# Output stage of full attention: gate folded into the output weights, normalising on ScalarE, loops written out

## The chip, the cores and the metric

The kernel runs on one core of a Trainium2 chip. The metric is the device time of one execution in microseconds, as the median of several runs. The engines are named as in the profile: PE is TensorE (PEld its weight loads), DVE is VectorE, ACT is ScalarE, POOL is GpSimd, and SP is SyncE, which here issues every DMA. PE's clock has two levels, 1.2 and 2.4 GHz; the profile gives the granted share.

## The reference

All is float32. B = 8 batches of N = 1024 tokens with D = 256 channels. The reference is a block with adaptive layer norm: full attention, then two layers of windowed attention with feed-forward. The change lies in the line that ends the full attention and in the norm behind it:

```python
mod = (_silu(c) @ wmod).reshape(8, 6, 1, -1)
sa, ca, ga, sb, cb, gb = (mod[:, i] for i in range(6))
ga = (2 * (ga >= 0) - 1) * jnp.maximum(jnp.abs(ga), 0.25)
h = _layernorm(x) * (1 + ca) + sa
x = x + ga * (softmax(q @ k.T / 4) @ v @ wo.T)   # attention(h), 16 heads of 16
h = _layernorm(x) * (1 + cb) + sb
```

Each batch b has one gate row ga[b] of 256 numbers, one scale row and one shift row, which are the rows 2, 4 and 3 of mod_d[b].

## The kernel before

The program is a chain of stages, each a block of its own with a barrier at its end: setup, projections, full_attention, attention_out, and then twice window_attention and feed_forward. The change lies in attention_out alone. It takes the attention's result att_d and the input x from memory, and writes x1 (the sum above) and the normalised, modulated h, in two halves lo and hi.

The tokens go through in NC = 16 chunks of 512 (CT = 4 tiles of 128 tokens, each 128 partitions by 256 channels); two chunks make a batch. For a chunk n:

- SP loads at (attention), xt (input) and mrow (three rows of mod_d, copied to all 128 partitions) into one of R = 4 buffers. After the first four chunks a load waits for POOL's last operation of chunk n - 4. SP then stores x1 when it is summed, and lo and hi when POOL is done.
- PE turns the attention (L1053, transposes, at to pT), ACT copies it out of PSUM (L1073, pT to aT), and PE multiplies by the output weights w["wo"] (L1061, to pY). pT, aT and pY have one buffer each: the product of chunk n waits until DVE has read pY of chunk n - 1, and the copy of chunk n until the product of chunk n - 1 is done.
- DVE multiplies pY by the gate row (L1085, gate) and adds the input (L1089, add). Both are placed inside the layer norm of the chunk before. That norm has steps chained by a semaphore: statistics (L364), aggregation (L369), variance plus epsilon (L371), then a reciprocal root by ten small steps on 128x4 values (L82, and three rounds of L84, L86, L87). After it come four normalising operations (L1101), one for each tile.
- POOL multiplies by the scale row and adds the shift row (L1136, twice 128x1024), from xn to hm.

The order on each engine is written by hand in body(n, r). On DVE that is: norm of chunk n up to the sixth step, gate of n + 1, two steps, add of n + 1, the last steps, normalize of n. The engines run four chunks written out, then an engine loop (Fori) of four chunks for each turn; DVE and SP also write out the last four.

Of the kernel before, what the change touches and what calls it, by code (L numbers as in the profile page):

```python
# [30 lines left out]
CT = 4  # L31
# [937 lines left out]
def attention_out(nc, x, ident, w, mod_d, att_d, x1_d, lo_dst, hi_dst):  # L969


    with ExitStack() as ctx:
# [15 lines left out]
        stats, mv = sb("ao_stats", [P, CT, 6]), sb("ao_mv", [P, CT, 2])  # L988
        ve, rstd, tmp = sb("ao_ve", [P, CT]), sb("ao_rstd", [P, CT]), sb("ao_tmp", [P, CT])
# [7 lines left out]
        gated = sig("gated", 2)  # L997
        chain = sig("chain", LN_INCS)
        normed = sig("normed")
# [9 lines left out]
        def drive(eng, body):  # L1009
            for n in range(R):  # L1010
                body(n, n)
            with eng.Fori(1, NC // R) as i:
                for r in range(R):
                    body(i * R + r, r)

        with nc.Block() as block:
            @block.sync
            def _(sp):
                def load(n, p):
                    if not isinstance(n, int):  # L1020
# [12 lines left out]

                for n in range(R):
                    load(n, n)
                with sp.Fori(0, NC // R - 1) as i:
                    for r in range(R):
                        store(i * R + r, r)
                        load(i * R + R + r, r)
                for n in range(NC - R, NC):  # L1040
                    store(n, n % R)
                for n in range(NC - R, NC):
                    sp.wait_ge(stored.sems[n % R], stored.upto(n))

            @block.tensor
            def _(pe):
                def body(n, r):
                    pe.wait_ge(loaded.sems[r], loaded.upto(n))
                    if again(n):
                        pe.wait_ge(aT_ready.sem, aT_ready.upto(n - 1))  # L1050
                    for t in range(CT):
                        for k in range(KT):
                            last = nc.tensor.transpose(pT[:, k, t * P:(t + 1) * P],  # L1053
                                                       at[:, r, t, k * P:(k + 1) * P], ident[:])
# [10 lines left out]
                drive(pe, body)  # L1065

            @block.scalar
            def _(act):
                def body(n, r):
                    act.wait_ge(turned.sem, turned.upto(n))  # L1070
                    if again(n):
                        act.wait_ge(projected.sem, projected.upto(n - 1))
                    nc.scalar.copy(aT[:], pT[:]).then_inc(aT_ready.sem, 1)  # L1073

                drive(act, body)

            @block.vector
            def _(dve):
                def gate(n, r):
                    dve.wait_ge(loaded.sems[r], loaded.upto(n))  # L1080
                    dve.wait_ge(projected.sem, projected.upto(n))
                    if not (isinstance(n, int) and n < R):
# [4 lines left out]
                def add(n, r):  # L1087
                    dve.wait_ge(gated.sem, gated.upto(n, 1))
                    nc.vector.tensor_tensor(x1[:, r], x1[:, r], xt[:, r], ALU.add).then_inc(gated.sem, 1)  # L1089

                def stats_of(n, r, steps):
                    if steps[0] == 0:
                        dve.wait_ge(gated.sem, gated.upto(n))
                    layer_norm_steps(nc, dve, chain, n, steps, x1[:, r], stats, mv, ve[:], rstd[:], tmp[:])

                def normalize(n, r):
                    dve.wait_ge(chain.sem, chain.upto(n))
                    if later(n):
                        dve.wait_ge(modded.sem, modded.upto(n - 2))
# [3 lines left out]
                    last.then_inc(normed.sem, 1)  # L1103

                def body(n, r, following=True):
# [10 lines left out]
                gate(0, 0)  # L1116
                add(0, 0)
                for n in range(R):
                    body(n, n)
                with dve.Fori(1, NC // R - 1) as i:  # L1120
                    for r in range(R):
                        body(i * R + r, r)
                for n in range(NC - R, NC):
                    body(n, n % R, following=n + 1 < NC)

            @block.gpsimd
            def _(pool):
                def body(n, r):
                    p = r % 2
                    pool.wait_ge(normed.sem, normed.upto(n))  # L1130
                    for t_in, t_out, row, op in ((xn, xn, 2, ALU.mult), (xn, hm, 1, ALU.add)):
                        if row == 1:
                            pool.wait_ge(modded.sem, modded.upto(n, 1))
                            if later(n):
# [3 lines left out]
                                                op).then_inc(modded.sem, 1)  # L1138

                drive(pool, body)  # L1140
# [939 lines left out]
```

## Time and profile before

| | us |
|---|---|
| median of 3 runs | 4590.83 |
| lowest and highest | 4581.98, 4592.19 |
| profiled execution, its own time | 4591.15 |
| its span in the trace | 4589.3 |
| attention_out in it, from the last DMA of the stage ahead to the first of the next | 1711.6 to 1901.7 |

The profiled execution's own time is 1.85 us more than its span and 0.3 us above the median. Over the whole program PE is busy for 91% of the span, DVE 79%, ACT 61% and POOL 35%; but these shares are means over stages of very different kinds, and attention_out is 4% of the span. So the stage has to be read by itself: the views of the trace are cut to its stretch, and times are counted from the span's start.

### The profile page before, as it was taken

The page shows a single profiled execution, that of the slowest core. Times are in us where ns is not written, and L with a number is a line of the kernel's source. Part 1 is how long each engine was busy: PE and PEld are TensorE (multiplying, and loading weights), DVE is VectorE, ACT ScalarE, POOL GpSimd, SP SyncE. Part 2 cuts the span into 40 slices and gives each one's busy share as a digit, 9 for nine tenths or more (in the row PEclk, how much of TensorE's full clock was granted, in tenths as well). Part 3 has the DMA queues.
Part 4 walks back from the last instruction along what each step waited for, and adds up shares of the span by engine and source line. Part 5 has one row for each costly group of instructions (what it writes and reads, how often), then busy time and mean ns, then how long its engine had stood idle before and what let it go on. Part 6 is the DMA issues. An engine that isn't in the chain of part 4 may idle for free. (4 is left out here: it accounts for less than half of the span.)

```text
span 4589.3 us, 81912 instructions
## 1 busy us (share of the span) xinstructions
PE 4160.5 (91%) x27034; PEld 2652.0 (58%) x27034; DVE 3603.7 (79%) x7996; ACT 2779.6 (61%) x6209; POOL 1597.4 (35%) x2408
## 2 busy tenths in 40 slices
PE   5959999999999976499999996999799999987998
PEld 2423333333333325377777775888577777766887
DVE  5679999999999938688888885565588888875665
ACT  1428888888888861166767664444467666653343
POOL 2400000000000003356555553444455555644555
PEclk8969999999999977799999998999899999998999
DMA  5943343343342307400000001111100000002221
GB/s 194 371 94 55 51 63 54 53 62 52 56 62 49 58 22 230 147 25 27 27 25 27 24 20 57 51 52 44 57 27 26 26 27 24 27 13 87 86 69 54
DMA packets 368553, 295.62 MB, mean 64 GB/s; under 512 B 66364, under 2 KB 325432, under 8 KB 368192
## 3 DMA queue, kind: packets, MB, share of 16 engines
q1 hardware_dynamic: 368192, 291.11, 25.8%
q8 instruction: 190, 3.11, 0.3%
q14 instruction: 171, 1.40, 0.1%
HBM read 178.74 MB, written 111.21 MB: 63 GB/s over the span
## 5 line engine op out<-in xcount | busy, mean ns | idle before, releaser
L885 ACT ACTIVATE fa_P<-fa_pS 128x512 f32<-128x512 f32 x2048 | 1111.8, 595 | 327.7 <-PE fa_pS L811 279.0
L912 DVE TENSOR_REDUCE fa_mx<-fa_pR 128x2 f32<-128x1024 f32 x1024 | 1205.6, 1221 | 92.4 <-PE fa_pR L792 78.0
L1519 POOL TENSOR_TENSOR wa_pn<-wa_pr,wa_ri 128x512 f32<-128x512 f32 (+1 forms) x512 | 673.4, 1315 | 506.9 <-DVE wa_ri L1576 506.3
L1452 ACT ACTIVATE wa_pr<-wa_sm,wa_mn 128x256 f32<-128x256 f32 (+1 forms) x1024 | 496.9, 488 | 172.1 <-DVE wa_mn L1567 149.5
L1136 POOL TENSOR_TENSOR ao_xn<-ao_xn,ao_mod 128x1024 f32<-128x1024 f32 x16 | 37.5, 2347 | 1598.7 <-DVE ao_xn L1101 1598.7
L826 PE MATMUL fa_pO<-fa_P,fa_V 128*32 128x512 f32 x4096 | 554.6, 614 | 0.0
L811 PE MATMUL fa_pS<-fa_Q,fa_K 50*128 50x512 f32 x2048 | 512.1, 497 | 41.5 <-ACT fa_P L885 11.2
L811 PEld LDWEIGHTS fa_pS<-fa_Q,fa_K 50*128 50x128 f32 x2048 | 192.8, 185 | 525.4 <-ACT fa_P L885 438.4
L792 PE MATMUL fa_pR<-fa_K,fa_Q 48*128 48x512 f32 x2048 | 430.1, 463 | 57.3 <-DMA fa_K<-parts_d 38.4
L1302 PE MATMUL wa_pQK<-wa_wqkv,wa_xT 128*128 128x512 f32 x1536 | 420.8, 410 | 6.3 <-DVE wa_qa L1613 6.3
L1567 DVE CUSTOM_DVE_ANT_0 wa_sm<-wa_pS,wa_mask 128x256 f32<-128x256 f32 (+1 forms) x1024 | 357.1, 403 | 21.3 <-issue 16.0
L1462 ACT COPY wa_pT<-wa_pP 128x512 f32<-128x512 f32 (+1 forms) x512 | 285.5, 558 | 127.3 <-PE wa_pP L1349 127.2
L1925 POOL TENSOR_TENSOR ff_u<-ff_uF,ff_u 128x512 fp32r<-128x512 f32 x192 | 246.7, 1289 | 307.3 <-ACT ff_u L2038 306.3
L2030 ACT ACTIVATE ff_gl<-ff_pG,ff_b 128x512 f32<-128x512 f32 x192 | 131.8, 687 | 355.9 <-PE ff_pG L1970 355.6
L792 PEld LDWEIGHTS fa_pR<-fa_K,fa_Q 48*128 48x128 f32 x2048 | 195.8, 188 | 247.1 <-DVE fa_mx L912 152.2
L1349 PE MATMUL wa_pP<-ident,wa_pn 128*128 128x128 f32 x1920 | 310.2, 282 | 15.1 <-ACT wa_pT L1462 10.9
L1970 PE MATMUL ff_pG<-ff_hT,ff_w 128*128 128x512 f32 x1152 | 302.6, 398 | 23.0 <-DVE ff_w L1899 23.0
L1302 PEld LDWEIGHTS wa_pQK<-wa_wqkv,wa_xT 128*128 128x128 f32 x1536 | 272.7, 191 | 54.0 <-DVE wa_qa L1613 7.7
L1336 PE MATMUL wa_pS<-wa_kT,wa_qT 64*128 64x256 f32 (+1 forms) x2048 | 277.0, 387 | 7.5 <-DVE wa_mn L1567 2.2
L1984 PE MATMUL ff_pY<-ff_w,ff_u 128*128 128x256 f32 x2304 | 279.7, 281 | 0.0
L1984 PEld LDWEIGHTS ff_pY<-ff_w,ff_u 128*128 128x128 f32 x2304 | 274.3, 188 | 0.2
L1361 PE MATMUL wa_pO<-wa_pT,wa_V 128*64 128x128 f32 x3840 | 268.4, 281 | 4.3 <-ACT wa_pT L1462 4.3
(186 smaller groups left out, 7058.7 us busy)
## 6 DMA issues: line engine op xcount, KB each, us to landing
parts_d<-pj_parts SPq DMA_DIRECT2D x64, 512.0 KB, 5.3
fa_Q<-parts_d SPq DMA_DIRECT2D x192, 128.0 KB, 4.5
fa_K<-parts_d SPq DMA_DIRECT2D x192, 128.0 KB, 7.4
v_d<-pj_v SPq DMA_DIRECT2D x16, 1024.0 KB, 8.4
fa_V<-v_d SPq DMA_DIRECT2D x32, 512.0 KB, 9.8
pj_x<-in_L_attn_x SPq DMA_DIRECT2D x16, 512.0 KB, 7.6
fa_Q<-fa_nrow SPq DMA_DIRECT2D x512, 2.0 KB
att_d<-fa_att SPq DMA_DIRECT2D x64, 128.0 KB, 2.3
```

The lines of the kernel that those rows point to most:

```text
L792: last = nc.tensor.matmul(slot[:, e, :], Qs[at:at + SROWS, s, a, q * P:(q + 1) * P], Ks[at:at + SROWS, s, a, kh * HALF:(kh + 1) * HALF], s ...
L811: nc.tensor.matmul(pS[:, (s * exped.per + u + e) % T, :], Ks[at:at + SROWS + 2, s, a, kb * P:(kb + 1) * P], Qs[at:at + SROWS + 2, s, a, ha ...
L826: last = nc.tensor.matmul(pO[h * 32:(h + 1) * 32, :], V[:, s, kb, h, :], Pr[:, k % 2, h, :], start=(kb == 0), stop=(kb == KB - 1))
L885: nc.scalar.activation(Pr[:, k % 2, h, :], pS[:, (s * exped.per + u) % T, :], ACT.Exp).then_inc(exped.sem, 1)
L912: nc.vector.tensor_reduce(mx[:, q // QB, :, a, q % QB, kh], row_slot(), AX.X, ALU.max).then_inc(row_free, 1)
L1302: last = nc.tensor.matmul(out, xT[:, x, k, :], wqkv[:, y, k, j * INNER:(j + 1) * INNER], start=(i == 0), stop=(i == len(products) - 1))
L1349: last = nc.tensor.transpose(pP[:, at:at + P], pn[:, hp % 2, hh, side * WIN:(side + 1) * WIN], ident[:])
L1452: last = nc.scalar.activation(pr[:, hp % 2, hh, lo:], sm[:, hp % 2, hh, lo:], ACT.Exp, bias=mn[:, p, h:h + 1], scale=-1.0, accum_out=rs[:, ...
L1519: nc.gpsimd.tensor_tensor(pn[:, hp % 2, :, lo:], pr[:, hp % 2, :, lo:], inv, ALU.mult).then_inc(s["weighted"].sem, 1)
L1567: last = nc.vector.tensor_tensor_reduce(out=sm[:, hp % 2, hh, lo:], in0=pS[:, hh, (hp % 2) * 2 * WIN + lo:(hp % 2 + 1) * 2 * WIN], in1=mas ...
L1970: last = nc.tensor.matmul(ps[:, j % 2, :], w1[:, x, k, part, j * P:(j + 1) * P], hT[:, p, y, k, :], start=(i == 0), stop=(i == len(product ...
L1984: last = nc.tensor.matmul(pY[:, t, :], u[:, x, j, t * P:(t + 1) * P], w2[:, y, j, :], start=(j == 0 and i == 0 and t % 2 == 0), stop=(j == ...
```

## The change

The gate row is multiplied into the output weights. One DMA at the start of the stage brings all eight gate rows to every partition (grow, 128 x 2048 numbers, 1 MB), and POOL makes wg, the weights of a batch times its gate row (weigh, 128x512), for two batches ahead of the chunks and then for one batch after each second chunk. PE's product reads wg in place of w["wo"] and also waits for it. DVE's gate is gone, and its add reads pY and xt. The load of mrow takes two rows in place of three.

The four normalising operations are gone from DVE. In their place one small operation (offset) makes shift = -mean * rstd, and ACT computes xn = rstd * x1 + shift in four activations of 128x256. On ACT they stand behind the copy of the next chunk: copy of n, then normalize of n - 1. mv, rstd and shift have two buffers.

All the engine loops of the stage are written out.

```diff
-        mrow = sb("ao_mod", [P, R, 3, D])
+        mrow = sb("ao_mod", [P, R, 2, D])
+        grow = sb("ao_gate", [P, B, D])
+        wg = sb("ao_wg", [P, 2, KT, D])
...
-        def drive(eng, body):
-            for n in range(R):
-                body(n, n)
-            with eng.Fori(1, NC // R) as i:
-                for r in range(R):
-                    body(i * R + r, r)
+        def drive(body):
+            for n in range(NC):
+                body(n, n % R)
...
-                    src = mod_d[bass.ds(n // 2, 1), 2:5, :].to_broadcast([P, 3, D])
+                    src = mod_d[bass.ds(n // 2, 1), 3:5, :].to_broadcast([P, 2, D])
...
+                sp.dma_start(grow[:], mod_d[:, 2, :].rearrange("(o b) c -> o b c", o=1).to_broadcast([P, B, D])
+                             ).then_inc(gates, 16)
...
+                    pe.wait_ge(weighed.sem, weighed.upto(n // 2))
                     if again(n):
-                        pe.wait_ge(gated.sem, gated.upto(n - 1, 1))
+                        pe.wait_ge(gated.sem, gated.upto(n - 1))
                     for t in range(CT):
                         for k in range(KT):
-                            last = nc.tensor.matmul(pY[:, t, :], aT[:, k, t * P:(t + 1) * P], w["wo"][:, k, :],
+                            last = nc.tensor.matmul(pY[:, t, :], aT[:, k, t * P:(t + 1) * P], wg[:, n // 2 % 2, k, :],
...
                     nc.scalar.copy(aT[:], pT[:]).then_inc(aT_ready.sem, 1)
+                    if n > 0:
+                        normalize(n - 1, (n - 1) % R)
+
+                def normalize(n, r):
+                    act.wait_ge(shifted_by.sem, shifted_by.upto(n))
+                    if n >= 2:
+                        act.wait_ge(modded.sem, modded.upto(n - 2))
+                    for t in range(CT):
+                        last = nc.scalar.activation(xn[:, r % 2, t, :], x1[:, r, t, :], ACT.Identity,
+                                                    bias=shift[:, r % 2, t:t + 1], scale=rstd[:, r % 2, t:t + 1])
+                    last.then_inc(normed.sem, 1)
...
-                    row = mrow[:, r, 0, :].unsqueeze(1).to_broadcast([P, CT, D])
-                    nc.vector.tensor_tensor(x1[:, r], pY[:], row, ALU.mult).then_inc(gated.sem, 1)
+                    nc.vector.tensor_tensor(x1[:, r], pY[:], xt[:, r], ALU.add).then_inc(gated.sem, 1)
...
-                    for t in range(CT):
-                        last = nc.vector.tensor_scalar(xn[:, r % 2, t, :], x1[:, r, t, :], mv[:, t, 0:1],
-                                                       rstd[:, t:t + 1], ALU.subtract, ALU.mult)
+                    nc.vector.scalar_tensor_tensor(out=shift[:, r % 2], in0=mv[:, r % 2, :, 0], scalar=-1.0,
+                                                   in1=rstd[:, r % 2], op0=ALU.mult,
+                                                   op1=ALU.mult).then_inc(shifted_by.sem, 1)
...
                     stats_of(n, r, range(0, 6))
-                    if following:
-                        gate(n + 1, (r + 1) % R)
-                    stats_of(n, r, range(6, 8))
-                    if following:
+                    if n + 1 < NC:
                         add(n + 1, (r + 1) % R)
-                    stats_of(n, r, range(8, LN_INCS))
-                    normalize(n, r)
+                    stats_of(n, r, range(6, LN_INCS))
+                    offset(n, r)
...
+                def weigh(b):
+
+                    if b >= 2:
+                        pool.wait_ge(projected.sem, projected.upto(2 * b - 3))
+                    nc.gpsimd.tensor_tensor(wg[:, b % 2], w["wo"][:], grow[:, b].unsqueeze(1).to_broadcast([P, KT, D]),
+                                            ALU.mult).then_inc(weighed.sem, 1)
```

How this moves instructions is seen best on two engines. On ACT, at the start of the stage, there stood copies alone before:

```order
L1073 COPY ao_aT<-ao_pT 128x1024 [waits ao_turned]
L1073 COPY ao_aT<-ao_pT 128x1024 [waits ao_projected,ao_turned] x3
```

Now it reads:

```order
L1077 COPY ao_aT<-ao_pT 128x1024 [waits ao_turned]
L1077 COPY ao_aT<-ao_pT 128x1024 [waits ao_projected,ao_turned]
L1086 ACTIVATE ao_xn<-ao_x,ao_shift,ao_rstd 128x256 [waits ao_shifted_by]
L1086 ACTIVATE ao_xn<-ao_x,ao_shift,ao_rstd 128x256 x3
L1077 COPY ao_aT<-ao_pT 128x1024 [waits ao_projected,ao_turned]
L1086 ACTIVATE ao_xn<-ao_x,ao_shift,ao_rstd 128x256 [waits ao_shifted_by]
```

The third copy (chunk 2) now stands behind the four activations of chunk 0, and these wait for DVE's offset of chunk 0 (the semaphore ao_shifted_by).

On DVE, the piece of the difference for one chunk (here chunk 1) from its first statistics on:

```order
 L364 BN_STATS ao_stats<-ao_x 128x6 x4
 L367 MEMSET ao_tmp 128x4
...
 L84 SCALAR_TENSOR_TENSOR ao_tmp<-ao_rstd 128x4
 L86 TENSOR_TENSOR ao_tmp<-ao_tmp,ao_ve 128x4
-L1085 TENSOR_TENSOR ao_x<-ao_pY,ao_mod 128x1024
+L1100 TENSOR_TENSOR ao_x<-ao_pY,ao_x 128x1024
 L87 SCALAR_TENSOR_TENSOR ao_rstd<-ao_tmp,ao_rstd 128x4
 L84 SCALAR_TENSOR_TENSOR ao_tmp<-ao_rstd 128x4
-L1089 TENSOR_TENSOR ao_x<-ao_x 128x1024
 L86 TENSOR_TENSOR ao_tmp<-ao_tmp,ao_ve 128x4
 L87 SCALAR_TENSOR_TENSOR ao_rstd<-ao_tmp,ao_rstd 128x4
```

The add of the next chunk (L1100) has come forward to where the gate stood, and seven small steps follow it. At the end of the chunk the four L1101 have given way to one:

```order
-L1101 TENSOR_SCALAR ao_xn<-ao_x,ao_mv,ao_rstd 128x256 x4
+L1112 SCALAR_TENSOR_TENSOR ao_shift<-ao_mv,ao_rstd 128x4
```

The next chunk's statistics stand directly behind it.

## Rows read from the trace of the kernel before

**Rows 1.** Busy time by stretch: stretch, length, engines, PEclk, DMA share, GB/s.

```profile
1771.00:1855.00 84.00, 52.07 (x195) 40.39 (x194) 78.14 (x210) 8.10 (x8) 37.73 (x17) 0.78 0.78 241
...
1711.00:1902.00 191.00, 101.00 (x384) 79.08 (x384) 153.03 (x419) 16.19 (x16) 75.14 (x32) 0.75 0.67 210
```

**Rows 2.** Groups of instructions, attention_out: count, busy us, mean ns, idle before.

```profile
L1061 PE MATMUL ao_pY<-woT,ao_aT 128*128 128x256 f32 x256 | 80.7, 484 | 32.9 <-DVE ao_x L1085 27.2 <-ACT ao_aT L1073 5.7
...
L84 DVE SCALAR_TENSOR_TENSOR ao_tmp<-ao_rstd 128x4 f32<-128x4 f32 x48 | 39.4, 822 | 1.9 <-DVE ao_rstd L82 0.3
L1136 POOL TENSOR_TENSOR ao_hm<-ao_xn,ao_mod 128x1024 f32<-128x1024 f32 x16 | 37.6, 2350 | 3.0 <-POOL ao_xn L1136 2.7
...
L1101 DVE TENSOR_SCALAR ao_xn<-ao_x,ao_mv,ao_rstd 128x256 f32<-128x256 f32 x64 | 22.1, 408 | 1.1 <-DVE ao_rstd L87 0.6
...
L1085 DVE TENSOR_TENSOR ao_x<-ao_pY,ao_mod 128x1024 f32<-128x1024 f32 x16 | 19.6, 1224 | 21.8 <-PE ao_pY L1061 19.8 <-issue 2.0
```

**Rows 3.** Timeline, DVE and POOL, chunks 0 to 2: start, duration, engine, line.

```profile
1736.49 1.22 DVE L1085 TENSOR_TENSOR ao_x<-ao_pY,ao_mod 128x1024 f32<-128x1024 f32 x1 [0.56 <-PE ao_pY L1061]
...
1737.63 0.15 DVE L87 SCALAR_TENSOR_TENSOR ao_rstd<-ao_tmp,ao_rstd 128x4 f32<-128x4 f32 x1
...
1739.81 0.16 DVE L87 SCALAR_TENSOR_TENSOR ao_rstd<-ao_tmp,ao_rstd 128x4 f32<-128x4 f32 x1
1740.01 1.38 DVE L1101 TENSOR_SCALAR ao_xn<-ao_x,ao_mv,ao_rstd 128x256 f32<-128x256 f32 x4
...
1741.47 2.36 POOL L1136 TENSOR_TENSOR ao_xn<-ao_xn,ao_mod 128x1024 f32<-128x1024 f32 x1 [1520.32 <-DVE ao_xn L1101]
...
1743.91 2.35 POOL L1136 TENSOR_TENSOR ao_hm<-ao_xn,ao_mod 128x1024 f32<-128x1024 f32 x1
1744.09 2.18 DVE L84 SCALAR_TENSOR_TENSOR ao_tmp<-ao_rstd 128x4 f32<-128x4 f32 x1
...
1751.37 2.35 POOL L1136 TENSOR_TENSOR ao_xn<-ao_xn,ao_mod 128x1024 f32<-128x1024 f32 x1 [5.11 <-DVE ao_xn L1101]
```

**Rows 4.** Timeline, PE, ACT and DVE, chunks 0 to 3.

```profile
1723.38 1.01 ACT L1073 COPY ao_aT<-ao_pT 128x1024 f32<-128x1024 f32 x1 [13.30 <-PE ao_pT L1053]
...
1724.44 6.25 PE L1061 MATMUL ao_pY<-woT,ao_aT 128*128 128x256 f32 x16 [1.10 <-ACT ao_aT L1073]
...
1730.80 1.22 DVE L1085 TENSOR_TENSOR ao_x<-ao_pY,ao_mod 128x1024 f32<-128x1024 f32 x1 [19.26 <-PE ao_pY L1061]
...
1741.92 1.04 PE L1053 MATMUL ao_pT<-ident,ao_att 128*128 128x128 f32 x8
...
1747.76 6.52 PE L1061 MATMUL ao_pY<-woT,ao_aT 128*128 128x256 f32 x16 [4.80 <-DVE ao_x L1085]
```

**Rows 5.** Timeline, PE, products of three chunks later in the stage.

```profile
1767.92 6.68 PE L1061 MATMUL ao_pY<-woT,ao_aT 128*128 128x256 f32 x16 [1.19 <-ACT ao_aT L1073]
...
1830.17 6.29 PE L1061 MATMUL ao_pY<-woT,ao_aT 128*128 128x256 f32 x16 [2.87 <-DVE ao_x L1085]
...
1840.70 3.72 PE L1061 MATMUL ao_pY<-woT,ao_aT 128*128 128x256 f32 x16 [2.73 <-DVE ao_x L1085]
```

**Rows 6.** ACT's groups over the whole span, the activation nearest in form.

```profile
L1452 ACT ACTIVATE wa_pr<-wa_sm,wa_mn 128x256 f32<-128x256 f32 x896 | 446.9, 502 | 148.6 <-DVE wa_mn L1567 148.6
```

**Rows 7.** Timeline of ACT in the last stage, scale and offset from tiles.

```profile
4550.55 0.77 ACT L2022 ACTIVATE ff_hT<-ff_pH,ff_lb,ff_lg 128x512 fp32r<-128x512 f32 x1
4551.22 0.78 ACT L2022 ACTIVATE ff_hF<-ff_pH,ff_lb,ff_lg 128x512 f32<-128x512 f32 x1
```

**Rows 8.** POOL's groups over the whole span, the one nearest to weigh.

```profile
L1519 POOL TENSOR_TENSOR wa_pn<-wa_pr,wa_ri 128x512 f32<-128x512 f32 x448 | 612.7, 1368 | 448.2 <-DVE wa_ri L1576 447.6
```

**Rows 9.** DMA view of 1700 to 1900 us: GB/s in 40 slices of 5 us.

```profile
GB/s 2 0 26 283 365 359 193 66 0 119 340 170 348 150 351 147 334 155 329 152 318 164 306 170 309 157 286 187 265 233 245 254 223 275 210 0 210 2 210 64
```

**Rows 10.** Timeline, start and end of the stage.

```profile
1721.37 1.97 PE L1053 MATMUL ao_pT<-ident,ao_att 128*128 128x128 f32 x8 [10.59 <-DMA ao_mod<-mod_d]
...
1893.03 2.34 POOL L1136 TENSOR_TENSOR ao_xn<-ao_xn,ao_mod 128x1024 f32<-128x1024 f32 x1 [3.08 <-DVE ao_xn L1101]
```

More of the change, by code:

```diff
@@ L996, in attention_out @@
         turned, aT_ready, projected = sig("turned"), sig("aT_ready"), sig("projected")
-        gated = sig("gated", 2)
+        gates = ctx.enter_context(nc.semaphore("ao_gates"))
+        weighed = sig("weighed")
+        gated = sig("gated")
         chain = sig("chain", LN_INCS)
+        shifted_by = sig("shifted_by")
         normed = sig("normed")
@@ L1019, in load @@
                 def load(n, p):
-                    if not isinstance(n, int):
+                    if n >= R:
                         sp.wait_ge(modded.sem, modded.upto(n - R))
@@ L1032, in store @@
                     sp.dma_start(padded(hi_dst, n, CH), hm[:, r % 2, :, P:D]).then_inc(stored.sems[r], 16)
+                sp.dma_start(grow[:], mod_d[:, 2, :].rearrange("(o b) c -> o b c", o=1).to_broadcast([P, B, D])
+                             ).then_inc(gates, 16)
                 for n in range(R):
                     load(n, n)
[L1036 to L1040, printed above, removed]
+                for n in range(NC):
                     store(n, n % R)
+                    if n + R < NC:
+                        load(n + R, n % R)
                 for n in range(NC - R, NC):
@@ L1073, in body, with add @@
                     nc.scalar.copy(aT[:], pT[:]).then_inc(aT_ready.sem, 1)
-                drive(act, body)
+                    if n > 0:
[8 more added lines that the diff above has]
+                    last.then_inc(normed.sem, 1)
+                drive(body)
+                normalize(NC - 1, (NC - 1) % R)
             @block.vector
             def _(dve):
-                def gate(n, r):
+                def add(n, r):
                     dve.wait_ge(loaded.sems[r], loaded.upto(n))
                     dve.wait_ge(projected.sem, projected.upto(n))
-                    if not (isinstance(n, int) and n < R):
+                    if n >= R:
                         dve.wait_ge(stored.sems[r], stored.upto(n - R))
-                    row = mrow[:, r, 0, :].unsqueeze(1).to_broadcast([P, CT, D])
-                    nc.vector.tensor_tensor(x1[:, r], pY[:], row, ALU.mult).then_inc(gated.sem, 1)
-                def add(n, r):
-                    dve.wait_ge(gated.sem, gated.upto(n, 1))
-                    nc.vector.tensor_tensor(x1[:, r], x1[:, r], xt[:, r], ALU.add).then_inc(gated.sem, 1)
+                    nc.vector.tensor_tensor(x1[:, r], pY[:], xt[:, r], ALU.add).then_inc(gated.sem, 1)
                 def stats_of(n, r, steps):
@@ L1093, in stats_of, with offset @@
                         dve.wait_ge(gated.sem, gated.upto(n))
-                    layer_norm_steps(nc, dve, chain, n, steps, x1[:, r], stats, mv, ve[:], rstd[:], tmp[:])
-                def normalize(n, r):
+                    layer_norm_steps(nc, dve, chain, n, steps, x1[:, r], stats, mv[:, r % 2], ve[:],
+                                     rstd[:, r % 2], tmp[:])
+                def offset(n, r):
                     dve.wait_ge(chain.sem, chain.upto(n))
-                    if later(n):
-                        dve.wait_ge(modded.sem, modded.upto(n - 2))
-                    for t in range(CT):
-                        last = nc.vector.tensor_scalar(xn[:, r % 2, t, :], x1[:, r, t, :], mv[:, t, 0:1],
-                                                       rstd[:, t:t + 1], ALU.subtract, ALU.mult)
-                    last.then_inc(normed.sem, 1)
@@ L1117, in _ @@
                 add(0, 0)
[L1118 to L1124, printed above, removed]
+                drive(body)
             @block.gpsimd
             def _(pool):
+                def weigh(b):
[3 more added lines that the diff above has]
+                                            ALU.mult).then_inc(weighed.sem, 1)
@@ L1128, in body @@
+                pool.wait_ge(gates, 16)
+                weigh(0)
+                weigh(1)
                 def body(n, r):
@@ L1130, in body @@
                     pool.wait_ge(normed.sem, normed.upto(n))
-                    for t_in, t_out, row, op in ((xn, xn, 2, ALU.mult), (xn, hm, 1, ALU.add)):
-                        if row == 1:
+                    for t_in, t_out, row, op in ((xn, xn, 1, ALU.mult), (xn, hm, 0, ALU.add)):
+                        if row == 0:
                             pool.wait_ge(modded.sem, modded.upto(n, 1))
@@ L1138, in body @@
                                                 op).then_inc(modded.sem, 1)
-                drive(pool, body)
+                    if n % 2 == 1 and n // 2 + 2 < B:
+                        weigh(n // 2 + 2)
+                drive(body)
 def window_signals(nc, ctx):
```

14 lines of the change are left out of this document (9 added, 5 removed).

## The prediction, on record before the result

> **What bounds the stage now.** First the busy time by stretch. In the middle of attention_out, 84 us long, DVE is busy for 78.1 us (93%), PE for 52, POOL for 38 and ACT for 8, and the DMA engines for 0.78 of the time [rows 1]. So DVE sets the pace there, and over the stage a chunk takes (1893.03 - 1741.47) / 15 = 10.1 us, from POOL's first operation to its last turn [rows 3, 10]; everything else waits for it: PE's products sat idle for 27.2 us of the stage until DVE had read pY [rows 2]. Next the groups. The dearest small thing on DVE is L84, a step on 128x4 values: 822 ns in the mean [rows 2], where its neighbours L87 take 0.15 to 0.16 us [rows 3]. The timeline shows why: the L84 that starts at 1744.09 takes 2.18 us and ends at 1746.27, with POOL's operation (1743.91 + 2.35 = 1746.26) [rows 3]. DVE's steps are held while POOL works, once in each chunk, for some 2 us. Last, PE's clock: the product of a chunk takes 3.72 us in some chunks and 6.3 to 6.5 in others [rows 4, 5]. All 16 take 80.7 us [rows 2]; eight of them are near 3.72, which leaves (80.7 - 29.8) / 8 = 6.36 for each of the other eight. The granted clock over the stage is 0.75 [rows 1], between the levels of 2.4 and 1.2 GHz. Now this costs nothing, since DVE is later anyway.
>
> **The change, read as removed work.** DVE loses the gate, 1.22 us, and four normalising operations, 1.38 us, and gains an offset of 0.16, the same kind of step as L87, which takes 0.15 to 0.16 [rows 2, 3]. By that alone a chunk would be 2.4 us shorter. But the order on ACT decides, not the sum on DVE.
>
> **The new ring.** Follow who waits for whom. DVE's offset of chunk n - 1 releases ACT's four activations of n - 1. Behind them on ACT stands the copy to aT of chunk n + 1, which releases PE's product of n + 1. That releases DVE's add of n + 1, which stands inside the norm of n, ahead of its last seven small steps and the offset of n. So from one offset to the next the chunk goes through all four engines in a row, and nothing in it can overlap. Before, ACT had only the copy, which waits for PE alone, so that the product ran while DVE was in its norm. The terms:
>
> - DVE's offset to ACT's start: 0.08, as from the end of L1101 (1740.01 + 1.38) to POOL's start at 1741.47 [rows 3].
> - Four activations of 128x256 with scale and offset from tiles, a form that the trace does not hold. Three rows bracket it: a copy of 1024 elements with no such operand takes 1.01 us [rows 4], 256 elements with one take 0.50 [rows 6], 512 with two take 0.77 to 0.78 [rows 7]. Taking a fixed part, a part for each element and one for each operand, the three give 0.23 us, 0.76 ns and 0.08 us, so 0.58 us for 256 elements with two. Of neighbours the second starts 0.10 before the first has ended (0.77 long, 0.67 apart) [rows 7], so I take 0.48 from one to the next: 4 x 0.48 = 1.92. The ends are 0.40 (0.50 less the 0.10, if the second operand costs nothing) and 0.60 (no overlap), 1.6 to 2.4 in all.
> - The copy, 1.01, and 0.05 from its end (1724.39) to PE's start at 1724.44 [rows 4].
> - The product: 3.72 or 6.36 us, weighed below.
> - From its end (1724.44 + 6.25 = 1730.69) to DVE's start at 1730.80: 0.11 [rows 4].
> - The add reads pY and xt as the gate read pY and a row; L87 starts 1.14 after it (1736.49 to 1737.63). Seven small steps lie 0.195 apart, 1.38 in all, and the offset takes 0.16 [rows 3]. Together 2.68.
>
> Without the product that is 0.08 + 1.92 + 1.01 + 0.05 + 0.11 + 2.68 = 5.85 us. PE does in this time only the transposes of the next chunk, 1.04 us right behind the product [rows 4], and then sits idle for 4.8 us. The trace of before has one such case: after an idle time of 4.80 us, with a product at full clock and transposes ahead of it, the product took 6.52 us [rows 4]. After 2.73 us one took 3.72, after 2.87 another took 6.29 [rows 5]. So the low clock is what I take for the ring, at the mean of the slow ones: **T = 5.85 + 6.36 = 12.2 us** a chunk, against 10.1 now.
>
> **Off the ring.** weigh is a POOL operation of 128x512, 1.37 us by the nearest row [rows 8]; POOL has two of 2.35 [rows 3] and half a weigh in each 12.2 us, and is free again 8.4 us after an offset (2.2 + 4.8 + 1.4), ahead of the add at 9.6. So both weigh and DVE's held steps in the first half of the norm hide behind copy and product; if the product is short, they do not (below). Each load waits for POOL some 7 us after its chunk's offset and is wanted when PE ends the product three chunks on, some 21 us after that offset; with a landing time of 6 to 8 us (chunk 0's took 7, from SP's first issue to 1721.37 [rows 10]) it is early, so the DMA waits of now go. The loops' going saves little: from POOL's first turn to its second, in written-out chunks, are 9.90 us (1741.47 to 1751.37) [rows 3], where the mean is 10.1; the ring's terms are taken from written-out chunks, so they have it already. The third row of mrow, 128 KB a chunk, saves nothing where no one waits for loads.
>
> **Start.** grow is 1.05 MB ahead of chunk 0's load, whose mrow is 0.13 MB less. At the 365 GB/s of the busiest slice [rows 9] the 0.92 MB take 2.5 us, so the first transposes come at 1723.9 instead of 1721.4 [rows 10]. The ends are 0.5 (its issue alone, if it runs beside) and 3.0. weigh for two batches is done meanwhile. The second product is not yet in the ring: its add falls at 1736.49 + 2.5, and the offset of chunk 0 ends 2.68 later, at 1741.7.
>
> **End.** The offset of chunk 14 comes 14 periods later. Chunk 15's norm has no add in it, but is held until POOL is through with chunk 14: 2.2 until the activations are done, 4.8 of POOL, then L86 and seven steps and the offset, 8.8 in all. After 2.2 more POOL starts on chunk 15, at 1741.7 + 14 T + 8.8 + 2.2 = 1752.7 + 14 T. Before it did so at 1893.03 [rows 10], and what follows (two POOL operations, the last stores, the barrier) is the same. T = 10.02 is the point at which nothing changes. With T = 12.21 it is 1923.6, or **30.6 us later**. Added to the profiled execution's own 4591.15 that is 4622; that execution lies 0.3 us above the median, so no correction is made.
>
> **A rule to weigh against rows.** The rows show DVE's L84 held until POOL's end [rows 3]. The Trainium skill (SBUF — State Buffer, Who interferes with whom) states a lock: a VectorE instruction with two SBUF inputs and a GpSimd instruction that reads SBUF exclude each other, and whoever issues first keeps the port; one SBUF input alone does not contend. By that rule weigh holds L86 up on every second chunk, while the new add, with one input from PSUM, goes through. In the ring at the low clock that changes nothing; it is the mechanism of the second rival below.
>
> **Rivals.**
>
> 1. *Mixed clock.* Idle times of 2.73 and 2.87 us left opposite clocks [rows 5], so one long idle time may not always bring the low level; against it stands the one row at 4.80. A turn with the product at 3.72 has T near 10 (see 2). If four to ten of the 14 turns are such, the stage gives back 2.2 each, 9 to 22 us: 4600 to 4613. The Trainium skill (TensorE: Matmul & The Clock Gate, Part 1) says that the gate's window runs freely, not from the first matmul; by it the same idle time can fall either way, which is this case.
> 2. *Full clock throughout, POOL's hold on the ring.* T by the ring is 5.85 + 3.72 = 9.57, but DVE's L84 is held until POOL ends 7.0 us after the offset, then L86, so the add starts at 7.2 and T is at least 9.9; with weigh in front of L86 on each second chunk it is 11.1 there. Mean 9.9 to 10.5: -2 to +7 us, 4589 to 4598. Against: PE's idle time would be 5 us or more here too.
> 3. *Faster.* Full clock throughout and DVE's steps ahead of POOL's operations rather than behind them: the ring is then 9.57, the last norm 5.4 instead of 8.8, the start 0.5 instead of 2.5. That is 1739.7 + 134.0 + 5.4 + 2.2 = 1881.3, 12 us earlier: 4579. It decides from T = 10.02 down, and needs the full clock in nearly all chunks and the steps ahead of POOL. The rows speak against both.
> 4. *The change does not do what it says:* the copies could overtake the activations. The order of instructions on ACT rules that out, since an engine takes them in turn; a part of it would look like 2.
>
> **How the numbers follow.** The forecast, low clock in nearly all turns, has 0.62: 4613 to 4632, where the upper end takes activations of 0.60 (+7) or a product of 6.68, the longest of before (+4) [rows 5]. Mixed clock 0.25, full clock with POOL 0.08, faster 0.05 with whatever else. The range of 4600 to 4632 holds the first two, with 0.13 and a little of the upper tail outside. A measurement of this kernel tells 0.2%, 9.2 us, from no change: from 4581.6 to 4600 is the same. That takes rival 2: same 0.08, faster 0.04, slower 0.88.
>
> **What would show it.** In the profile after: PE's product of most chunks at 6 us or more, ACT's copy directly behind four activations, PE waiting for the copy and DVE's add for the product, each in every chunk; offsets 12.2 us apart; a stage of some 220 us instead of 190; granted clock at or under 0.7; no wait of PE for loads after the first; POOL's holds on DVE still there, but ahead of the add's wait. Wrong would be: adds that start right behind L86 without a wait (the ring not closed or not the bound), a period of 10 us, or products at 3.72.

## The result, and the profile after

| | before | after |
|---|---|---|
| median of 5 runs, us | 4590.83 | 4610.22 |
| lowest and highest | 4575.17, 4592.19 | 4596.28, 4616.46 |
| profiled execution, its own time | 4591.15 | 4596.28 |
| attention_out in it, from DVE's last operation of the stage ahead to the first DMA of the next | 190.1 | 213.9 |
| POOL's first operation of a chunk, first to 15th chunk, for each of the 14 turns | 10.26 | 11.70 |

The changed kernel is slower: the ratio of the times is 1.0056, with a 95% interval of 1.0036 to 1.0075, or 16 to 34 us. The median, 4610, lies inside the forecast range of 4600 to 4632 and 12 us below the forecast of 4622.

The two profiled executions are only 5 us apart, though the stage alone grew by 23.8. The rest is in code that is the same in both: in the execution after, the last group of full_attention ran 13.6 us shorter (it is shown at the end), and the stages behind attention_out 5.0 us shorter (2682.6 against 2687.7). So the stage is read from its own two ends and never from the total of a single execution.

The busy time by stretch for the kernel after, in the same columns as [rows 1] (stretch, length, PE, PEld, DVE, ACT, POOL, PEclk, DMA share, GB/s); the second is the whole stage:

```profile
1771.00:1855.00 84.00, 49.26 (x182) 39.54 (x180) 48.64 (x155) 20.78 (x35) 37.48 (x18) 0.80 0.66 202
...
1697.00:1912.00 215.00, 107.05 (x386) 85.77 (x384) 110.03 (x355) 47.73 (x80) 85.14 (x40) 0.75 0.59 182
```

DVE, which was busy for 78 of these 84 us, is now busy for 49. None of the engines PE, DVE, ACT and POOL is busy for more than 60%, and the DMA share fell too, from 0.78 to 0.66. ACT is busier than before, 21 us against 8, and still mostly idle. When every engine is idle for over 40% of the time and the stage is longer, the time has gone into waits of one for another. The groups of the stage name them (columns as in [rows 2]):

```profile
L1065 PE MATMUL ao_pY<-ao_wg,ao_aT 128*128 128x256 f32 x256 | 91.8, 536 | 71.5 <-ACT ao_aT L1077 71.5
...
L1086 ACT ACTIVATE ao_xn<-ao_x,ao_shift,ao_rstd 128x256 f32<-128x256 f32 x64 | 33.2, 588 | 135.0 <-DVE ao_shift L1112 135.0
...
L1100 DVE TENSOR_TENSOR ao_x<-ao_pY,ao_x 128x1024 f32<-128x1024 f32 x16 | 19.6, 1225 | 87.1 <-PE ao_pY L1065 87.1
```

ACT waits for DVE's offset (135.0 us), PE for ACT's copy (71.5), DVE's add for PE's product (87.1, of which 22.8 before the first chunk). Each waits for the one ahead of it, in a circle. Before, PE's product waited for DVE [rows 2], while DVE, after its wait of 19.26 us for the first product [rows 4], waited for PE hardly at all: 19.8 us in the whole stage [rows 2]. One turn of the circle, from the timeline of all engines for chunks 0 to 2:

```profile
1728.99 0.16 DVE L1112 SCALAR_TENSOR_TENSOR ao_shift<-ao_mv,ao_rstd 128x4 f32<-128x4 f32 x1
...
1729.19 2.08 ACT L1086 ACTIVATE ao_xn<-ao_x,ao_shift,ao_rstd 128x256 f32<-128x256 f32 x4 [6.58 <-DVE ao_shift L1112]
...
1731.17 0.99 ACT L1077 COPY ao_aT<-ao_pT 128x1024 f32<-128x1024 f32 x1
...
1731.34 2.37 POOL L1149 TENSOR_TENSOR ao_xn<-ao_xn,ao_mod 128x1024 f32<-128x1024 f32 x1 [22.09 <-ACT ao_xn L1086]
1731.53 2.20 DVE L86 TENSOR_TENSOR ao_tmp<-ao_tmp,ao_ve 128x4 f32<-128x4 f32 x1
...
1732.21 5.41 PE L1065 MATMUL ao_pY<-ao_wg,ao_aT 128*128 128x256 f32 x16 [4.96 <-ACT ao_aT L1077]
...
1737.72 1.22 DVE L1100 TENSOR_TENSOR ao_x<-ao_pY,ao_x 128x1024 f32<-128x1024 f32 x1 [4.00 <-PE ao_pY L1065]
...
1740.23 0.16 DVE L1112 SCALAR_TENSOR_TENSOR ao_shift<-ao_mv,ao_rstd 128x4 f32<-128x4 f32 x1
```

From offset to offset are 1740.23 - 1728.99 = 11.24 us. The circle is offset, activations, copy, product, add, and each of them begins within 0.1 us of the end of the one ahead of it; between the add and the next offset stand only DVE's seven small steps. PE sat idle for 4.96 us before the product, and in the 13 turns that follow it is the same, 4.94 to 4.96 each time. The products of the 14 turns take 5.11 to 6.75 us, 5.89 in the mean, and none takes 3.72; the last one of the stage in the timeline of PE:

```profile
1883.52 6.75 PE L1065 MATMUL ao_pY<-ao_wg,ao_aT 128*128 128x256 f32 x16 [4.95 <-ACT ao_aT L1077]
```

PE's clock, read in the idle time ahead of a product and in the product itself, for these two turns (columns as above):

```profile
1727.31:1732.21 4.90, 0.00 (x0) 0.00 (x1) 4.47 (x22) 2.97 (x5) 0.87 (x1) 1.00 0.00 0
1732.21:1737.62 5.41, 5.41 (x18) 4.40 (x19) 1.52 (x1) 0.00 (x0) 3.83 (x2) 0.68 0.10 27
1878.62:1883.52 4.90, 0.00 (x1) 0.00 (x1) 4.48 (x22) 2.97 (x5) 0.87 (x1) 0.93 0.39 130
1883.52:1890.27 6.75, 6.75 (x16) 5.09 (x16) 1.51 (x1) 0.00 (x0) 3.83 (x2) 0.54 0.29 81
```

The granted clock is 1.00 or nearly so while PE is idle, and 0.68 and 0.54 in the products behind. So a mean over a stretch hides the loss: in the 84 us above the clock is 0.80, where before it was 0.78 [rows 1]. What shows the loss is the length of the products.

DVE's held step stands in the turn too: L86 at 1731.53 takes 2.20 us while POOL's operation of 1731.34 runs, and has no one waiting for it.

### The profile page after: what moved, and what is told of

Read it like the earlier page. It is cut to its first block and busy times, and to the rows that moved or that the text cites. A ratio compares the mean times of both kernels' runs of the same rounds, so it can differ in the third digit from the quotient of the medians.

```text
span 4594.5 us, 81577 instructions
## 1 busy us (share of the span) xinstructions
PE 4148.6 (90%) x27034; PEld 2652.2 (58%) x27034; DVE 3556.0 (77%) x7932; ACT 2812.2 (61%) x6273; POOL 1613.9 (35%) x2416
## 5 line engine op out<-in xcount | busy, mean ns | idle before, releaser
L1134 POOL TENSOR_TENSOR ao_wg<-woT,ao_gate 128x512 f32<-128x512 f32 x8 | 10.1, 1265 | 1486.4 <-DMA ao_gate<-mod_d 1486.4
L1582 DVE CUSTOM_DVE_ANT_0 wa_sm<-wa_pS,wa_mask 128x256 f32<-128x256 f32 (+1 forms) x1024 | 357.2, 403 | 19.0 <-issue 13.8
L1985 PE MATMUL ff_pA<-ff_hT,ff_w 128*128 128x512 f32 x960 | 253.8, 400 | 18.5 <-DVE ff_uF L1875 18.5
```

The source lines that it names most:

```text
L1582: last = nc.vector.tensor_tensor_reduce(out=sm[:, hp % 2, hh, lo:], in0=pS[:, hh, (hp % 2) * 2 * WIN + lo:(hp % 2 + 1) * 2 * WIN], in1=mas ...
L1985: last = nc.tensor.matmul(ps[:, j % 2, :], w1[:, x, k, part, j * P:(j + 1) * P], hT[:, p, y, k, :], start=(i == 0), stop=(i == len(product ...
```

## The experiments

What each kernel says is read from the stage in its profile, in the same way for all. "Turn" is the mean of 14 turns, from POOL's first operation on the first chunk to that on the 15th. The stage runs from DVE's last operation of full_attention to the first DMA of the next stage.

| kernel | stage, us | turn, us | products of the 14 turns, us |
|---|---|---|---|
| before | 190.1 | 10.26 | 3.72 and 6.06 to 6.68 |
| after | 213.9 | 11.70 | 5.11 to 6.75 |
| e1, copy ahead of activations | 177.2 | 9.10 | 3.7 and 5.1 to 6.7 |
| e2, fold alone | 179.8 | 9.34 | 3.7 and 5.4 to 6.5 |
| e3, ScalarE's part alone | 230.2 | 13.05 | 5.1 to 6.8 |
| e4, PE filled | 183.8 | 9.58 | 3.72, all |
| e5, weights first | 213.8 | 11.74 | 5.1 to 6.8 |
| e7, loops written out alone | 184.3 | 9.95 | 3.7 and 5.3 to 6.6 |
| e9, e1 with PE filled | 176.2 | 9.05 | 3.6 to 4.1 |
| e10, e1 with early loads | 172.9 | 8.82 | 3.7 and 5.2 to 6.6 |
| e12, e10 with weights first | 166.4 | 8.38 | 3.7 and 5.3 to 5.9 |
| e11, e12 with PE filled | 165.8 | 8.39 | 3.6 to 3.7 |

Each stage in this table is from one execution. How far it varies by itself was not measured; after and e5 agree to 0.1 us. Of e1 to e10 there is no other execution: their whole times are 4565.97, 4575.68, 4619.27 and 4575.80 us for e1 to e4, where before took 4577.90 on the same chip, and 4600.07, 4579.16, 4562.97 and 4560.17 for e5, e7, e9 and e10, where before took 4598.83. They carry the spread that is shown at the end, so the stage decides.

**e1: the order on ACT.** The theory was the circle; the rival, that the loss came from the work moved to POOL and ACT. The edit moves no work, only the place of the activations:

```diff
-                    if n > 0:
-                        normalize(n - 1, (n - 1) % R)
+                    if n > 1:
+                        normalize(n - 2, (n - 2) % R)
...
                 drive(body)
+                normalize(NC - 2, (NC - 2) % R)
                 normalize(NC - 1, (NC - 1) % R)
```

> The changed kernel with one thing moved: on ACT the copy of chunk n + 1 stands ahead of the activations of chunk n - 1 (copy of n, then normalize of n - 2). Work is the same. Ring theory: the copy no longer waits for DVE's offset, so the ring of 11.7 us a chunk is open; the period falls to what DVE and POOL need together, 8 to 10 us, and the stage from 213.9 us to 160 to 190. PE no longer waits for the copy but for DVE's add. Rival (the loss comes from the work put on POOL and on ACT, or from the clock by itself): the order on ACT changes nothing, the period stays at 11 us or more.

Measured: the turn fell to 9.10 us and the stage to 177.2, 36.7 less than after and 12.9 less than before. With the order on ACT put right the whole loss is gone. One point of the expectation missed: PE does not wait for DVE's add but in part for loads. Its waits from 1740 to 1870 us:

```profile
PE ao_pT L1056 <- DMA ao_mod<-mod_d: 25.0, 7, 5.6
...
DVE ao_x L1101 <- PE ao_pY L1065: 16.2, 6, 4.7
```

(Waiter, waited for: us in total, times, the longest.) Normalising comes one chunk later, so POOL is done later, and the load four chunks on, which waits for POOL, starts later.

**e2: the fold alone.** Here the normalising goes back to DVE; the folded gate and the written-out loops stay.

```diff
-                    if n > 0:
-                        normalize(n - 1, (n - 1) % R)
...
-                    nc.vector.scalar_tensor_tensor(out=shift[:, r % 2], in0=mv[:, r % 2, :, 0], scalar=-1.0,
-                                                   in1=rstd[:, r % 2], op0=ALU.mult,
-                                                   op1=ALU.mult).then_inc(shifted_by.sem, 1)
+                    for t in range(CT):
+                        last = nc.vector.tensor_scalar(xn[:, r % 2, t, :], x1[:, r, t, :], mv[:, r % 2, t, 0:1],
+                                                       rstd[:, r % 2, t:t + 1], ALU.subtract, ALU.mult)
+                    last.then_inc(normed.sem, 1)
```

> The changed kernel with the normalising put back on DVE (four operations of 128x256 in place of the offset); the gate stays in the weights, the loops stay written out. Ring theory: ACT has only copies, so no ring; DVE's 9.9 us of a written-out chunk before, less the gate of 1.14, give 8.8 us a chunk, or up to 9.5 if weigh holds DVE; stage 165 to 178 us. Rival (folding the gate costs more than it gives, by weigh on POOL and the DMA of 1 MB): the period stays above 10 us.

Measured: 9.34 us a turn, inside what was expected, and 179.8 for the stage, 1.8 above it. The fold is a gain of its own. Against the loops alone (e7, 9.95) it is 0.61 us a turn, not the 1.14 of the gate. A part of what is missing shows in the groups of this kernel:

```profile
L86 DVE TENSOR_TENSOR ao_tmp<-ao_tmp,ao_ve 128x4 f32<-128x4 f32 x48 | 13.9, 290 | 1.6
```

L84 is held as before, 796 ns in the mean where [rows 2] have 822, and now L86 is at 290 ns in the mean where 160 is its free time: 6.2 us in 16 chunks, 0.4 us each, by POOL's weigh. That agrees with the rule of the Trainium skill weighed in the prediction (SBUF — State Buffer, Who interferes with whom), since L86 has two inputs in SBUF.

**e3: ScalarE's part alone.** The gate goes back to DVE, with no folded weights and no extra DMA; the activations stay on ACT in the changed order.

```diff
-                            last = nc.tensor.matmul(pY[:, t, :], aT[:, k, t * P:(t + 1) * P], wg[:, n // 2 % 2, k, :],
+                            last = nc.tensor.matmul(pY[:, t, :], aT[:, k, t * P:(t + 1) * P], w["wo"][:, k, :],
...
                     if n + 1 < NC:
+                        gate(n + 1, (r + 1) % R)
+                    stats_of(n, r, range(6, 8))
+                    if n + 1 < NC:
                         add(n + 1, (r + 1) % R)
-                    stats_of(n, r, range(6, LN_INCS))
+                    stats_of(n, r, range(8, LN_INCS))
```

> The changed kernel with the gate put back on DVE (no weights times gate, no extra DMA, three rows in mrow, gate and add in two operations); normalising stays on ACT in the changed order. Ring theory: the ring stands and holds one operation more: gate, two steps, add and the rest, 1.0 us above the changed kernel's 5.82 without the product, so 12.7 us a chunk with a product of 5.9, stage about 225 us. Rival (the fold is what costs): the period falls below 11.7.

Measured: 13.05 us a turn, a third of a microsecond above the forecast, all of it in longer products (6.2 in the mean), and 230.2 for the stage, 5 above it. The half of the change that moves work to ScalarE is the harmful one; the fold shortens the circle that it makes.

**e4: the clock.** The work of PE grows by eight products of 128x256 in each chunk from the third on, whose output nobody reads.

```diff
+        pD = ctx.enter_context(nc.psum_tensor("ao_pD", [P, D], F32))
...
                     last.then_inc(turned.sem, 1)
+                    if n >= 2:
+                        for k in range(8):
+                            nc.tensor.matmul(pD[:], ident[:], w["wo"][:, k % 2, :], start=True, stop=True)
                     pe.wait_ge(aT_ready.sem, aT_ready.upto(n))
```

> The changed kernel with eight more products of 128x256 on PE behind each chunk's transposes, into a PSUM bank that nobody reads, so that PE is busy for some 3.7 of the 4.95 us in which it sat idle. It adds work and removes none. Ring theory with the clock: the real product falls from 5.9 to 3.72 us and the period from 11.7 to 9.6, or 9.8 to 10.3 if POOL's operations then hold DVE's steps on the ring; stage 184 to 195 us. Rival (the low clock does not come from the idle time): products stay at 5 us or more and the period at 11.7 or above.

Measured: all products at 3.72, 9.58 us a turn, 183.8 for the stage, 0.2 below what was expected. The groups of its stage:

```profile
L1069 PE MATMUL ao_pY<-ao_wg,ao_aT 128*128 128x256 f32 x256 | 61.8, 396 | 23.6 <-ACT ao_aT L1081 23.6
L1062 PE MATMUL ao_pD<-woT,ident 128*128 128x256 f32 x224 | 50.7, 379 | 0.0
```

50.7 us of useless products took 30 us off the stage, and the granted clock from 1771 to 1855 us is 1.00, where after has 0.80. The clock gave back 2.17 us a turn, from 5.89 to 3.72, and 9.58 - 3.72 = 5.86 is what the forecast had for all the rest. So e1 and e4 each take away the whole loss, by different ends: the order makes the circle, the circle leaves PE idle, and the low clock behind the idle time makes the circle longer than the old chunk of 10.26. POOL's hold did not come onto the circle, as the lower of the two forecasts said.

**e5: weigh's place.** All eight weights are made ahead of the chunks.

```diff
-        wg = sb("ao_wg", [P, 2, KT, D])
+        wg = sb("ao_wg", [P, B, KT, D])
...
-                weigh(0)
-                weigh(1)
+                for b in range(B):
+                    weigh(b)
...
-                    if n % 2 == 1 and n // 2 + 2 < B:
-                        weigh(n // 2 + 2)
```

> The changed kernel with all eight products of weights and gate made by POOL at the start of the stage (eight buffers), none among the chunks. Ring theory: POOL's weigh ends ahead of DVE's add in each turn, so it is off the ring; the period stays at 11.7 us give or take 0.2 (the clock), the stage at 214 us; the start is not later, since the weights of batch 0 still come first. Rival (weigh holds DVE's steps on the ring on every second chunk): the period falls by 0.5 us or more, the stage by 7 or more.

Measured: 11.74 and 213.8, no change. Within the circle weigh is hidden.

**e7: the loops alone.** The kernel before, with its engine loops in this stage written out.

```diff
-            for n in range(R):
-                body(n, n)
-            with eng.Fori(1, NC // R) as i:
-                for r in range(R):
-                    body(i * R + r, r)
+            for n in range(NC):
+                body(n, n % R)
```

> The kernel before with one edit: the engine loops of the stage written out, nothing else changed. From the trace of before, where written-out chunks take 9.9 us and those in the loop 10.4 to 10.6: the period falls from 10.1 to 9.9, the stage from 190.5 us to 186 to 188. Rival (register work and branches of the loops are hidden behind the engines' waits): no change within 1 us.

Measured: 9.95 us a turn, 184.3 for the stage, 5.8 less than before and 1.7 below what was expected. It is the third part of the change and a gain as well. So against before the loops give 0.31 us a turn, the fold 0.61 more (e2), and the activations, placed as they are, cost 2.37.

**e9 and e10: what bounds e1.** Two suspects, the clock and the late loads, one taken away in each. e9 adds four of the products of e4 to e1. e10 changes SP's order in e1, where load now issues the attention and the input alone and load_rows the two mod rows:

```diff
                     sp.dma_start(rows(x1_d, n), x1[:, r]).then_inc(stored.sems[r], 16)
+                    if n + R < NC:
+                        load(n + R, r)
                     sp.wait_ge(modded.sem, modded.upto(n))
...
-                        load(n + R, n % R)
+                        load_rows(n + R, n % R)
```

> The copy-first order (copy of n, then normalize of n - 2) with four more products of 128x256 behind each chunk's transposes, into a bank that nobody reads. In the copy-first run the period was 9.10 us, with products of 3.72 and 5.1 to 6.7 us in turn. If the clock sets a part of that: the slow products go, the period falls to 8.2 to 8.8. If the loads set it (PE waited 25 us for them there, since a load waits for POOL's last operation four chunks back, which now comes later): products at 3.72 but the period at 9.0 or above.

> The copy-first order with SP's loads of attention and input for chunk n + 4 issued when DVE has read chunk n, in place of after POOL's last operation on it; only the two mod rows still wait for POOL. If the loads set the pace of the copy-first order: PE's waits for DMA fall from 25 us, mostly to the mod rows' landing, and the period from 9.10 to 8.3 to 8.9. If the clock sets it: period within 0.2 of 9.1.

Measured: e9 has its products at 3.6 to 4.1 and still 9.05 us a turn; the clock is not what bounds the open order. e10 has 8.82, as forecast, and its waits from 1740 to 1870 us name the next thing:

```profile
PE ao_pY L1070 <- POOL ao_wg L1140: 18.5, 6, 3.6
...
DVE ao_x L1106 <- PE ao_pY L1070: 2.3, 4, 1.0
```

weigh, hidden in the circle, is waited for as soon as the circle is open: it stands behind two chunks' work on POOL. But the second line says that PE's wait hardly reaches DVE: DVE waited for the product only 2.3 us in these 130. The timeline of DVE and POOL shows where weigh does cost:

```profile
1780.11 1.26 POOL L1140 TENSOR_TENSOR ao_wg<-woT,ao_gate 128x512 f32<-128x512 f32 x1
1780.20 1.18 DVE L84 SCALAR_TENSOR_TENSOR ao_tmp<-ao_rstd 128x4 f32<-128x4 f32 x1
```

A step of 0.16 us is held until weigh ends, on every second chunk.

**e12 and e11: all together.** e12 is e10 with the weights made first as in e5; e11 adds the four products of e9. Both were timed in several executions, beside the kernel before.

> Copy-first order, early loads, and all weights times gate made at the start. In the early-loads run PE waited 18.5 us for POOL's weigh in six chunks; that wait goes. If it was on the path, the period falls from 8.82 to 8.0 to 8.5 and the stage from 172.9 to 162 to 169 us; if DVE and POOL bound each other anyway, by the steps held, the period stays within 0.2 of 8.8. Against the kernel before the stage is 20 to 28 us shorter, the time 4562 to 4575 where before has 4590.

> As the run beside it, with four more products of 128x256 on PE behind each chunk's transposes into a bank that nobody reads. If PE's clock still costs anything, the period falls by 0.2 to 0.6 us more; if DVE and POOL set the pace, it stays within 0.1 of the run beside it.

Measured: e12 has 8.38 us a turn and a stage of 166.4, with a median of 4567.02 against 4588.9 for before on the same chip, ratio 0.9957 (0.9944 to 0.9971). e11 has 8.39 and 165.8, 4562.94, ratio 0.9947 (0.9928 to 0.9966). The two cannot be told apart, so the clock costs nothing that can be seen there: DVE in e12 waited for PE only 0.4 us in 120.

The period fell as the first branch of the expectation said, but not for its reason. From e10 to e12 DVE's waits for PE could give at most some 2 us. L84 fell from 336 ns in the mean to 206 (47 of them, 6.1 us), and 14 turns became 6.1 us shorter: what weigh cost was its hold on DVE, not PE's wait for it.

Yet DVE's chunk of 8.38 us is not all work. The timeline of DVE and POOL in e12 shows it:

```profile
1805.57 2.36 POOL L1153 TENSOR_TENSOR ao_xn<-ao_xn,ao_mod 128x1024 f32<-128x1024 f32 x1 [3.58 <-ACT ao_xn L1091]
1805.76 2.19 DVE L86 TENSOR_TENSOR ao_tmp<-ao_tmp,ao_ve 128x4 f32<-128x4 f32 x1
1807.88 1.21 DVE L1106 TENSOR_TENSOR ao_x<-ao_pY,ao_x 128x1024 f32<-128x1024 f32 x1
...
1808.01 2.35 POOL L1153 TENSOR_TENSOR ao_hm<-ao_xn,ao_mod 128x1024 f32<-128x1024 f32 x1
1809.01 1.37 DVE L87 SCALAR_TENSOR_TENSOR ao_rstd<-ao_tmp,ao_rstd 128x4 f32<-128x4 f32 x1
```

L86 loses 2.03 us to POOL's first operation and L87 1.2 to its second, while the add between them, with one input in PSUM, runs beside the second at its usual 1.21. Without the two holds, 3.24 us together, a chunk would take DVE some 5.1 us, an estimate from these rows. That these holds set the 8.38 us is read from the trace and was not tried by itself.

## Why the prediction was right, and where it was off

The mechanism was as forecast: the circle over four engines, a product slowed by the low clock in each turn, PE's loads no longer waited for (its only wait for a DMA is the first one). e1 shows that the order on ACT makes the circle, e4 that with PE's idle time filled the low clock is gone. The number alone would not have shown this: 4610 lies in the band of 4600 to 4613 that rival 1 had, some products at full clock, and not in the 4613 to 4632 of the forecast's own case. The products decide, and none was at full clock. The sum, term by term, with POOL's first operation on chunk 15 counted from the end of full_attention:

| term | forecast | measured |
|---|---|---|
| start, to POOL's first operation (29.9 before) | 32.4 | 33.4 |
| a turn without the product | 5.85 | 5.82 |
| the product | 6.36 | 5.89 |
| 14 turns | 170.9 | 163.9 |
| the last norm | 8.8 | 8.2 |
| all, against before | +30.6 | +23.9 |

**The product was mis-sized, and it is the whole miss in the stage:** 14 x 0.47 = 6.6 us of 6.7; the other terms cancel. The rest of the 12 us between 4622 and the median is not in the stage and lies within the spread of executions. The mean of the slow products of before, 6.36, was taken over. In the ring most turns had 5.41 or 5.11 and the others 6.45 to 6.75. PE is idle for the same 4.95 us in each (4.8 forecast), so the idle time alone does not fix the length. The clock does: granted in the product were 0.72 where it took 5.11, 0.68 where 5.41, 0.57 where 6.45, 0.55 where 6.65 and 0.54 where 6.75. In the six turns with 5.41 the clock was at 1.00 through the idle time and fell only when the product had begun; in the others it fell shortly before, 0.87 to 0.94 in the idle time. The slow products of before were not the same case. Ahead of three of them the transposes had waited 2.8 to 4.3 us for a load and ran for 1.97 us at a clock of 0.50, so the low clock was there before the product; in the ring the transposes take 1.04. Nor were the idle times of 2.73 and 2.87 us [rows 5] alike: the transposes ahead of the first had waited 0.42 us, those ahead of the second 2.86. What sets the moment at which the clock falls no run shows. That the Trainium skill (TensorE: Matmul & The Clock Gate, Part 1) has the gate's window run freely fits a spread at equal idle times, but the mix that rival 1 made of it, some products at 3.72, did not occur in any of the 14. The marks that the prediction set for this were too strict too: products of 6 us or more in most chunks (six of 14 were) and a granted clock at or under 0.7 (0.75 over the stage, the same as before).

**The activations** were worked out from three rows of other shapes as 0.58 us and 0.48 apart; they take 0.588, and four with the copy's start behind them 1.98 us, against 1.92. Each handover was right to 0.04, and DVE's tail took 2.67 against 2.68.

**The start** was put at 2.5 us for the DMA of the gate rows. From DVE's last operation of full_attention to PE's first transposes are 9.8 us before and 14.0 after, 4.1 more; e3 and e7, without that DMA, have 9.6 and 9.4. The upper end given was 3.0, so the bound by the busiest slice's rate was too low. The first product was faster by 0.6 in that execution (5.69 against 6.25), so a good part of it did not show.

**The last norm** was held by POOL less than forecast, 8.2 against 8.8, because three of DVE's small steps (an L86, an L87 and an L84) fell into POOL's time, held or between its two operations, and not behind it as reckoned.

**The rivals.** POOL's hold on the ring at full clock (rival 2) would have given at least 9.9 us a turn. e4 made that case, and it was 9.58: with the activations in between, POOL's first operation starts 2.2 us after the offset, when L84 is past; only L86 is held, and it is free 2.2 us before the product ends. So at full clock the change would have come out near rival 3's ring of 9.57, a stage 6 us shorter than before. The 23.8 us lost, and the 6 not gained, are what e4 gave back with the order left as it was.

## What to carry to other kernels

Before moving work to an idle engine, write down what stands behind it in that engine's order and whom that serves: if the moved work waits for the end of a chunk and the work behind it feeds the start of a later chunk, the engines form a circle, and the period is the sum round it however idle they are. The remedy needs no added work: let the work that feeds others go first and lag the moved work by one more chunk; then look at what the lag delays (here the loads, and after them the weights). The wait that a view names for one engine need not be what the pace hangs on: look whether it reaches the engine that sets the pace (PE's 18.5 us for weigh reached DVE with 2.3). And where a circle leaves PE idle, reckon a part of its product at the low clock, here 5.11 to 6.75 us in place of 3.72, and read it from the products and not from the mean clock of a stretch.

## What the runs showed of the hardware

The total of a single execution carries a spread that has nothing to do with the change. In full_attention's last group PE has no row scores of a following group to work on. In the profiled execution of before it had a granted clock of 0.65 in the same 36 us in which that of after had 1.00. The columns are those of the first rows above; first before:

```profile
1661.00:1697.00 36.00, 29.02 (x124) 7.46 (x124) 0.68 (x2) 22.43 (x43) 0.00 (x0) 0.65 0.03 8
```

and after:

```profile
1661.00:1697.00 36.00, 26.71 (x170) 7.69 (x170) 0.68 (x2) 28.71 (x54) 0.00 (x0) 1.00 0.03 8
```

Both had reached this point at the same time (the third store from the last was issued at 1660.88 and 1660.78), and DVE's last operation ended at 1711.53 and 1697.95. The experiments fell anywhere between, in the order of their clock in these 36 us: 1697.7 to 1700.2 with 1.00, 1704.6 with 0.90 (e7), 1706.0 with 0.86 (e2), 1711.4 with 0.74 (e11). The code of that group is the same in all, so 13.8 us of spread go with whether PE keeps the clock in it; that is over half of what the change itself cost.
